# Feed-forward of an audio tower: the second product two sequences behind the first, idle products ahead of a wait

## What is computed

```python
h = _L0_tok_ref(x, ...)                       # top-k tokens
h = h + _L0_attn_ref(_layernorm(h), ...)
h = h + _L0_ffn_ref(_layernorm(h), ...)       # the part that is changed
h = h + _L1_attn_ref(_layernorm(h), ...)
h = h + _L1_ffn_ref(_layernorm(h), ...)

def _L0_ffn_ref(x, W1, b1, W2, b2, s_gelu, s_out):
    h = einsum(x, _quant_weight(W1)) + b1     # 192 -> 768: the "hidden" (first) product
    h = gelu(h)
    h = _fq(h, s_gelu, -128, 127)             # round and clip
    y = einsum(h, _quant_weight(W2)) + b2     # 768 -> 192: the second product
    return _fq(y, s_out, -128, 127)

def _L1_attn_ref(x, ...):
    scale = max(max(abs(x)) / 127, 1e-8)      # one maximum over all 16 sequences
    ...
```

## Time and profile before

| | us |
|---|---|
| three runs: median | 1282.94 |
| lowest and highest of them | 1281.63, 1284.97 |
| the profiled execution | 1281.29 |
| its span in the trace | 1279.6 |
| TensorE busy | 1081.3 |
| VectorE busy | 1072.5 |
| ScalarE busy | 996.7 |
| GpSimd busy | 857.4 |

### The profile page before, as it was taken

The page is one execution under the profiler, slowest core; times in us unless marked ns, Lnnn a source line. Parts: engine busy times, 40 slices in busy tenths (PEclk is TensorE's granted clock), DMA queues, the critical chain, the costliest instruction groups (busy, mean ns, idle before and its releaser), DMA issues. The chain is left out here.

```text
span 1279.6 us, 44047 instructions
## 1 busy us (share of the span) xinstructions
PE 1081.3 (85%) x18872; PEld 824.9 (64%) x18875; DVE 1072.5 (84%) x2070; ACT 996.7 (78%) x902; POOL 857.4 (67%) x932
## 2 busy tenths in 40 slices
PE   4967878888788788788878877998999999998796
PEld 3644655666566566566656655997567777776595
DVE  8889999999999999999999998588566777788342
ACT  3489999999999999999999999686345555544242
POOL 3099899898889889888988989676011223334354
PEclk9999999999999999999999999998999999999898
DMA  5799999940000000000000000110000200002451
GB/s 161 237 360 359 358 340 330 335 135 11 11 2 11 10 10 4 11 11 2 12 10 3 11 11 3 50 26 1 2 3 3 69 20 19 19 14 62 133 156 45
DMA packets 78547, 107.84 MB, mean 84 GB/s; under 512 B 6963, under 2 KB 76489, under 8 KB 78356
## 3 DMA queue, kind: packets, MB, share of 16 engines
q1 hardware_dynamic: 67894, 91.62, 21.9%
q0 software_dynamic: 5360, 8.02, 2.0%
q10 hardware_dynamic: 5104, 5.43, 1.5%
HBM read 18.32 MB, written 83.85 MB: 80 GB/s over the span
## 5 line engine op out<-in xcount | busy, mean ns | idle before, releaser
L1031 ACT ACTIVATE work<-work 128x2864 f32<-128x2864 f32 (+1 forms) x272 | 681.3, 2598 | 4.9 <-POOL work L452 4.7
L452 POOL TENSOR_TENSOR work<-shared 128x1253 f32<-128x1253 f32 (+1 forms) x272 | 612.1, 2268 | 79.2 <-PE psum L2074 68.0
L2074 PE MATMUL psum<-work,ws_place 128*32 128x179 f32 x8640 | 395.2, 322 | 138.0 <-ACT work L1031 112.9
L452 DVE TENSOR_TENSOR work<-psum,shared 128x1611 f32<-128x1611 f32 (+3 forms) x288 | 488.0, 1722 | 1.0 <-PE psum L2074 0.4
L2074 PEld LDWEIGHTS psum<-work,ws_place 128*32 128x32 f32 x8640 | 269.3, 111 | 229.6 <-ACT work L1031 174.4
L2279 PE MATMUL psum<-shared 32*32 32x179 f32 (+1 forms) x3456 | 99.1, 326 | 1.2 <-DVE peaks L1682 0.7
L1407 DVE SCALAR_TENSOR_TENSOR p_sb<-psum,bs_col,s_top 128x358 f32<-128x358 f32 x144 | 82.1, 570 | 15.0 <-PE psum L2086 0.2
L920 POOL DMA_INDIRECT xs_dram<-w_store,slot_i x24 | 28.5, 1188 | 81.0 <-DVE slot_i L1782 74.8
L2086 PE MATMUL psum<-ident,p_sb 128*128 128x128 f32 x416 | 77.7, 294 | 1.1 <-ACT pt_region L1017 1.1
L1404 DVE TENSOR_REDUCE s_top<-psum 128x2 f32<-128x358 f32 x144 | 71.5, 496 | 5.5 <-PE psum L2074 5.4
L2086 PEld LDWEIGHTS psum<-ident,p_sb 128*128 128x128 f32 x416 | 43.5, 142 | 42.3 <-issue 33.4
(11 more groups left out here) (445 smaller groups left out, 2023.7 us busy)
## 6 DMA issues: line engine op xcount, KB each, us to landing
xs_dram<-pad_row SPq DMA_DIRECT2D x23, 3088.0 KB, 28.6
pt_region<-xs_dram SPq DMA_DIRECT2D x19, 193.0 KB, 2.4
pt_region<-xs_dram ACTq DMA_DIRECT2D x19, 193.0 KB, 2.8
xs_dram<-pad_row SPq DMA_DIRECT2D x1, 2895.0 KB, 28.4
pt_region<-v_sb SPq DMA_DIRECT2D x22, 96.0 KB
work<-in_x SPq DMA_DIRECT2D x2, 768.0 KB, 9.8
work<-in_x ACTq DMA_DIRECT2D x2, 768.0 KB, 12.5
work<-in_L_ffn_W2T SPq DMA_DIRECT2D x1, 1536.0 KB
```

The source lines that it names most:

```text
L452: ins = eng.tensor_tensor(dst[:, a * KEEP:e * KEEP].rearrange("p (u s) -> p u s", s=KEEP), k[:, h * KP:h * KP + KEEP].unsqueeze(1).to_broa ...
L1031: act.activation(a, a, ACT.Tanh).then_inc(tanh_done, 1)
L2074: ins = pe.matmul(bank_s[p % 2][32 * quad:32 * quad + 32, at:at + KEEP], ws_place[:, j, :], arg_slot(n)[:, u * KEEP:(u + 1) * KEEP], start ...
```

## The change

In the feed-forward TensorE's second product in step i is that of sequence i-2 and not i-1. Its buffer of `hq` is then the one of the same parity as the step. The loop reaches two steps behind and not one, so there is one step more at the end (step 17). The wait for `resid_added` moves from step 1 to step 2, where the first second product now is. The programs of the other engines are unchanged. After the feed-forward the wait for `qv_blank` 4 moves from ahead of the idle products to just ahead of the transpose of the maximum, and the first group of idle products has 22 in place of 24.

```diff
             def ffn_out(i, par):
 
-                if real(i - 1):
-                    b = i - 1
+                if real(i - 2):
+                    b = i - 2
                     pe.wait_ge(hq_ready, b + 1)
...
-                            ins = pe.matmul(bank[:, t * D:(t + 1) * D], hq[1 - par][:, c, t * TA:t * TA + TA], w2q[:, c, :],
+                            ins = pe.matmul(bank[:, t * D:(t + 1) * D], hq[par][:, c, t * TA:t * TA + TA], w2q[:, c, :],
                                             start=(c == 0), stop=(c == HT - 1))
...
-                if isinstance(i, int) and i == 1:
+                if isinstance(i, int) and i == 2:
                     pe.wait_ge(resid_added, 2 * B)
                 ffn_out(i, par)
...
-            staged(pe, ffn_step, (1, 1))
+            staged(pe, ffn_step, (1, 2))
...
             pe.wait_ge(w1_loaded, 16 * 21)
-            pe.wait_ge(qv_blank, 4)
             pe.wait_ge(small1, 2)
             pe.wait_ge(y_step, B - 1)
-            warm_up(24)
+            warm_up(22)
             pe.wait_ge(f_added, B)
             pe.wait_ge(n3_step, B - 2)
             warm_up(9)
             pe.wait_ge(x_maxed, 1)
+            pe.wait_ge(qv_blank, 4)
             pe.transpose(bank_k0[:, 0:128], x_max[:, 0:1].to_broadcast([128, 128]), ident[:, :]).then_inc(x_alled, 1)
```

## The result

| | before | changed |
|---|---|---|
| median of 20 runs, us | 1282.99 | 1285.05 |
| lowest and highest, us | 1281.55, 1284.97 | 1282.31, 1287.40 |
| span of the profiled execution, us | 1279.6 | 1284.6 |

The changed kernel takes 1.0015 of the time before (95% interval 1.0008 to 1.0022), so 1.9 us more (1.0 to 2.8). That is inside 0.3% and on the side that was forecast: 1284.6 was predicted. How much of that nearness is luck is said further down.

What follows compares the result with a forecast made beforehand. TensorE's own work was taken as the bound in the feed-forward. The profiled 1281.3 us, + 2.1 up to the transpose, + 0.8 at the head, gave 1284.2, with a quarter of the median's excess 1284.6; range 1281.8 to 1287.4.

Steps and rivals of the forecast that it cites:

- The moved wait: Behind the feed-forward: idle products no longer wait for the blanks, so the transpose follows VectorE's maximum; gains 3.7 us at most.
- Steady part: Feed-forward loop: step stays 5.09 us, one turn late behind a norm blocked by a memset; +0.26 us, bounds 0 and 2.8.
- slack of 0.59 us: Feed-forward steps: what VectorE's norm has left before its turn, claimed to shrink from more than a step to 0.59 us.
- Blocked rounds: VectorE's rounds in the loop: POOL memsets slide off them, leaving 0.1 to 0.5 us of blocking, under the slack.
- Head: Feed-forward start: TensorE's idle grows from 1.55 to 2.5 us and the clock may fall; +0.8 us, bounds 0 and 2.2.
- Tail: Feed-forward end: last second product +4.9 us later, at half clock +1.0, VectorE's chain to the maximum -0.3.
- My 2.9: The whole predicted change: transpose 2.1 us later, plus 0.8 at the start of the feed-forward.
- the 0.4: Quarter carried of the 1.65 us by which the median exceeds the profiled execution, taking 1284.2 to 1284.6.
- (a): Rival: clock holds at the feed-forward's start and in the last second product; +1.1 only, 1282.4 (1282.8 with the quarter); chance 0.22.
- (b): Rival: VectorE becomes the bound, turns wait for norms; 1288.8, or 1286.7 with six POOL periods alone; chance 0.14.
- (c): Rival: the later second product's cost at the end is hidden and the moved wait brings 3.5; 1277.8; chance 0.04.
- (d): Rival: idle products behind the wait still end last, transpose 2.6 to 3.0 us later; 1285.5 with the quarter; chance 0.12.

Runs made afterwards that it cites:

- the gap filled: Kernel before with only the wait moved, plus 8 idle products in TensorE's gap ahead of the last second product; 0.9972 of before, -3.6 us.
- the delayed kernel before: Kernel before with four unused reductions (1.9 us in all) at the end of VectorE's step 8; no turn moved, profile stage 86.65 us.
- the changed kernel with VectorE delayed: Changed kernel with four unused reductions (1.9 us in all) at the end of VectorE's step 8; one turn 1.94 us late, profile stage 91.61 us.
- the kernel with the head filled: Changed kernel with 10 idle products in TensorE's idle stretch ahead of turn 3; 1.0004 of before, +0.5 us.
- the lag alone: Kernel before with the second product two sequences behind, wait for the blanks and 24 idle products left as before; 1.0043 of before, +5.5 us.
- the tail filled: Changed kernel with 8 and 12 idle products ahead of the last two second products; 1.0012 of before, +1.5 us.
- the wait alone: Kernel before with only the wait for the blanks moved behind 22 idle products, second product still one sequence behind; 0.9961 of before, -5.0 us.
- first one early: Changed kernel with only the first second product back in step 1, all others two sequences behind; 0.9990 of before, -1.3 us.

## Why the prediction was right

**The moved wait (up to 3.7, nearly all of it used).** Right. Maximum to read was 4.23 us and is 0.60, so 3.63 us. Alone it is 3.2 us in the profiles (3.8 with the gap filled) and 3.3 to 6.5 in the comparison, 2.1 to 5.3 with the gap filled.

**Steady part (+0.26).** Right that there is no gain and that TensorE stays the bound: the step is 5.09 us throughout. The slack of 0.59 us is what the profile shows (0.74 less 0.15), and the delayed kernel before shows that it was more than a step there. The 0.15 itself was read at a turn that had to wait for TensorE's own products (they end at 813.93 + 0.99 = 814.92, where turn 3 starts) and not for the norm; it came out right all the same: the turn that did wait for its norm, in the changed kernel with VectorE delayed, stands 0.13 behind it (857.81 + 1.37 = 859.18 against 859.31). Only turn 3 stands further behind its norm, 0.26 in the changed kernel (817.33 against 817.59). The 0.26 itself was mis-sized: from turn 3 to the last hidden product's end the changed kernel's second profile has 69.85 us and the one before 69.81. I had kept the long memset on the norm of sequence 5; it now falls on the round ahead of it (2.44 us at 821.37 in the changed kernel's second profile, where the memset runs from 820.58 to 823.24), and the turn still comes in time. In the kernel with the head filled, that turn was late by 0.13.

**Blocked rounds (0.1 to 0.5 left).** Right in kind: none of the rounds beside the memset of L801 is long any more (0.72 at 851.18), the adds beside it keep 0.62. The rule of the Trainium skill ("SBUF — State Buffer", section "SBUF: two separate sides"), by which an operation with two SBUF inputs contests the shared port pair only against a GpSimd operation that reads, agrees with the add at 850.65 (L1545), which keeps its 0.62 us inside the memset of 849.83 to 851.21.

**Head (+0.8, bounds 0 and 2.2).** Right. The clock fell in three of the five profiles with the unfilled head (the changed kernel, the lag alone, the changed kernel with VectorE delayed) and held in two (the changed kernel again, the tail filled). Each fall costs 5.78 - 4.12 = 1.7 us, so 1.0 in the mean of these five. So it is all or nothing, and 0.8 was a mean of the two; that it came near the mean of five profiles is in part luck, as there was one row for each side. That the longer idle is the cause is likely by the count (three of five against none of seven) and not shown beyond it. Ahead of turn 3, and so outside the stage, the head costs another 0.1: from the attention's last products to turn 3 it was 814.92 - 810.82 = 4.10 us and is 817.59 - 813.38 = 4.21.

**Tail (+4.9, +1.0, -0.3).** From the last hidden product's end to the last second product it was 888.08 - 884.73 = 3.35 and is 7.79 to 7.81: +4.45, where 4.9 less the steady 0.26 is 4.64. The 0.2 between is the round that was blocked before and is not now (0.95 us at 882.43 before, 0.72 at 891.47 now). From that product's start to the add 2.21 and not 1.27: +0.94. From add to maximum 7.53 and not 8.04: -0.5.

The sum for an execution with the clock held at the head: 4.45 + 0.04 + 0.94 - 0.51 - 3.63 = 1.29, and the profiles give 87.99 - 86.70 = 1.29. With 1.0 for the head that is 2.3, and 1.9 (1.0 to 2.8) was measured. My 2.9 was 0.6 too high: 2.1 in place of 1.3 up to the transpose (0.2 each in the steady part, in the blocked round and in VectorE's last chain, 0.1 each in the last second product and in the moved wait), and 0.2 too little for the head.

That 1284.6 lies within 0.5 of the measured median of 1285.05 is partly luck. I added the 2.9 to the profiled execution, which lies 1.7 under the median of the kernel before, and put only 0.4 of that back. On the full median the same 2.9 would have made 1285.9. The base was 1.3 too low and the change about 1 too high. My ground for the 0.4, the clock's return inside the idle products, is not borne out either: the second profile before is 1.4 us longer (1281.0 against 1279.6), and all but 0.1 of that comes behind the read of the maximum.

**The rivals.** (a), the clock held, is what single executions show at the head, but in none of the unfilled tails. (b) did not come: behind turn 3 no turn of the changed kernel waits for a norm in either profile; one is 0.13 late with the head filled, and one waits when VectorE is delayed. (c) fails at the tail, as argued. (d) is where I was most wrong: I priced the wait in its old place, beside the lag, as 0.5 to 0.9 us worse than moved. It is 3.6 to 3.9 worse, because about 12 of the 33 idle products behind the wait run at half clock (2.5 us), and the changed kernel itself came out 0.8 us better up to its transpose. I had counted all of them at full clock, though I had worked out 9.4 at half clock for the kernel before, behind the same wait; with these, 2.0 us more, (d) would have been 2.5 to 2.9 worse. It did not touch the forecast, but it hid how much of the change's result the moved wait carries.

In sum the change is a loss of 5.5 us (the lag, 3.8 to 7.1) and a gain of 3.6 (the moved wait beside it). The gain stands alone: the wait alone is the better kernel.

## What to carry to other kernels

When the bounding engine has no idle inside a loop, a deeper lag on it gains nothing there and is paid at both ends: one more item behind the last of the loop, with the other engine's whole chain between, and one less to fill the wait at the head. Before lengthening a pipeline, count its slack step by step, and ask what the items did in the idle stretch that they leave. A wait ahead of idle products defeats them: put products whose result nobody reads ahead of every wait that they do not need, and look whether the engine has its clock when they begin.

## What the runs showed of the hardware

The same idle of 2.64 us ahead of turn 3 was followed by half clock in one execution of the same kernel and by full clock in another. At the tail the clock was at half when the last second product began in all six profiles of the kernels with the lag whose tail was not filled, and where the idle products followed at once, it came back 2.7 us behind that product's start (changed kernel, 899.5) to 5.2 us (first one early, 899.3 after 894.09). The Trainium skill ("TensorE: Matmul & The Clock Gate", Part 1) says that the transition point, there that of the rise to full clock, varies from run to run, and these rises vary too; a fall that comes in one execution and not in another is not what that sentence is about.

With an idle of 2.37 us between the half-clock second product and the idle products (lag alone), TensorE was at half clock until some 5 us into the second burst (898.48 to 903.6), 9.6 us behind the start of the last second product. That is one profile.

The attention, 800 us of code without a change, ended 2.7 us apart in two executions of one kernel (817.59 and 814.87). Of the 5.0 us between the two first profiles over half came from there, so two profiles can be compared only from a common point near the edit.
